# A decoder layer stack: softmax sums of the first attention taken from the value products, and plain downward products in the last expert stage

## The reference, cut to what matters

```python
# first sub-layer: 16 heads of 8 values, B = 4 batches, T = 512 tokens
qkv = layernorm(x) @ W_attn + b_attn                      # q, k, v
att = einsum('bqhd,bkhd->bhqk', q, k) * scale / temperature
att = where(causal, att + slope[h] * (k_pos - q_pos), -inf)
w = softmax(att)                                          # exponentials divided by their sum
x = x + einsum('bhqk,bkhd->bqhd', w, v) @ W_proj + b_proj
...
# last sub-layer: 32 experts of width 64, 4 for each token, the weights are given in bfloat16
h = silu(xe @ W1) * (xe @ W3)
ye = h @ W2                                               # the downward product
x = x + sum over experts of weight * ye + silu(x @ sw1.T) * (x @ sw3.T) @ sw2.T
```

## Time and profile before

| | us |
|---|---|
| median of three runs | 2444.63 |
| lowest, highest | 2435.88, 2444.8 |
| the profiled execution | 2446.44 |
| its span | 2444.7 |

### The profile page before, as it was taken

The page is one execution under the profiler, slowest core; times in us unless marked ns, Lnnn a source line. Parts: engine busy times, 40 slices in busy tenths (PEclk is TensorE's granted clock), DMA queues, the critical chain, the costliest instruction groups (busy, mean ns, idle before and its releaser), DMA issues. The chain is left out here.

```text
span 2444.7 us, 37814 instructions
## 1 busy us (share of the span) xinstructions
PE 2141.9 (88%) x12822; PEld 1482.2 (61%) x12822; DVE 1735.3 (71%) x3653; ACT 1214.2 (50%) x2508; POOL 1174.9 (48%) x1354
## 2 busy tenths in 40 slices
PE   6998779578999976658999999999999977869888
PEld 3666557455788854455666666666666645548655
DVE  5778678655788865665777777778766764479498
ACT  6888545223566652234444444544444433444455
POOL 5332028001699940117766776667665610004298
PEclk8999889867999988768999999999999998989899
DMA  1000015000766600012442434333433331000184
GB/s 49 2 3 2 7 48 123 7 6 21 172 154 153 155 21 20 1 68 39 89 102 74 105 72 106 76 102 82 93 91 73 83 78 41 0 1 1 41 180 108
DMA packets 64904, 161.92 MB, mean 66 GB/s; under 512 B 7995, under 2 KB 19003, under 8 KB 57416
## 3 DMA queue, kind: packets, MB, share of 16 engines
q1 hardware_dynamic: 64712, 159.50, 27.7%
HBM read 156.46 MB, written 3.01 MB: 65 GB/s over the span
## 5 line engine op out<-in xcount | busy, mean ns | idle before, releaser
L2361 PE MATMUL bank<-l2h_og,l2h_wo 128*128 128x512 f32 x512 | 260.2, 593 | 1.6 <-DVE LNT L2622 1.6
L2471 ACT ACTIVATE l2h_pr<-twin,l2h_nmx 128x512 f32<-128x512 f32 x256 | 176.0, 688 | 152.1 <-PE bank L2350 105.4
L2463 ACT ACTIVATE l2h_prT<-bank 128x512 f32<-128x512 f32 x256 | 151.6, 592 | 195.0 <-PE bank L2350 195.0
L1177 POOL TENSOR_TENSOR l1m_hid_lo<-l1m_hid,l1m_hid_hi 128x512 fp32r<-128x512 f32 x128 | 209.5, 1657 | 46.4 <-ACT l1m_hid_hi L1110 46.1
L2625 DVE TENSOR_REDUCE l2h_nmx<-twin 128x2 f32<-128x1024 f32 x128 | 156.0, 1219 | 93.3 <-PE twin L2339 93.2
L2700 POOL TENSOR_TENSOR l2h_vs<-l2h_vg 128x256 f32<-128x256 f32 x256 | 192.9, 753 | 20.3 <-DVE l2h_vg L2598 20.3
L2598 DVE TENSOR_TENSOR l2h_vg<-bank,l2h_gv 128x512 f32<-128x512 f32 x256 | 174.6, 682 | 34.4 <-POOL l2h_vs L2700 21.8
L2610 DVE TENSOR_TENSOR l2h_og<-bank,l2h_gt 128x512 f32<-128x512 f32 x256 | 172.8, 678 | 3.8 <-PE bank L2361 2.7
L2695 POOL TENSOR_TENSOR l2h_plain<-l2h_plain,l2h_rotated 128x512 f32<-128x512 f32 x64 | 82.5, 1289 | 172.9 <-DVE l2h_rotated L2591 172.9
L2350 PE MATMUL bank<-ident,l2h_pr 128*128 128x128 f32 x1024 | 160.8, 280 | 0.0
L2350 PEld LDWEIGHTS bank<-ident,l2h_pr 128*128 128x128 f32 x1024 | 116.7, 140 | 66.8 <-issue 43.1
(11 more groups left out here) (608 smaller groups left out, 5940.1 us busy)
## 6 DMA issues: line engine op xcount, KB each, us to landing
l2h_gt<-l2m_gate_rows SPq DMA_DIRECT2D x128, 512.0 KB, 7.4
l1m_c<-l1m_weights SPq DMA_DIRECT2D x62, 512.0 KB, 6.5
l3m_c<-l3m_weights SPq DMA_DIRECT2D x30, 512.0 KB, 6.6
l0m_c<-l0m_weights SPq DMA_DIRECT2D x14, 512.0 KB, 6.7
l1m_w<-in_l1m_pairs SPq DMA_DIRECT2D x32, 192.0 KB, 6.5
l2h_fresh<-in_l2m_wqkv SPq DMA_DIRECT2D x8, 768.0 KB, 4.3
l2h_wo<-in_l2m_wo SPq DMA_DIRECT2D x8, 512.0 KB, 3.8
l0m_w<-in_l0m_pairs SPq DMA_DIRECT2D x8, 192.0 KB, 5.7
```

What stands on the lines that cost most here:

```text
L1177: nc.gpsimd.tensor_tensor(hid_lo[:, h % RING, :], hid[:, h % 4, :], hid_hi[:, h % RING, :], ALU.subtract)\
L2361: nc.tensor.matmul(ybank[:, :], wo[s][:, e, :], og[:, e % 4, :], start=(e == 0), stop=(e == E - 1))\
L2463: nc.scalar.activation(prT[:, j // 2 % 2, h, :, j % 2 * P:(j % 2 + 1) * P], tbank[:, :].rearrange("p (c q) -> p c q", c=TPB), ACT.Copy).th ...
L2471: nc.scalar.activation(pr[:, h, :], sbank[:, h, :], ACT.Exp, bias=nmx[:, k % 2, h:h + 1], accum_out=rs[:, g % 2, t, h:h + 1]).then_inc(exp ...
```

## The change

In the first attention:

- The cell of a head in `v` is now 32 columns wide (8 values, 8 ones, 16 zeros). One product of 32 columns gives both the weighted values and the sums, and L494 is gone. Groups 0 and 1 go to the first 128 columns of `obank`, groups 2 and 3 to the second.
- After each fourth quad, ScalarE copies `obank` to `raw_y`, three iterations after the quad. VectorE no longer inverts and multiplies there.
- Once for each batch, in iterations 2 to 6 of the next: TensorE picks the sums (`sum_rows`, 8 products, iteration 2), VectorE inverts 64 columns and spreads them to 1024 (iteration 3), TensorE brings the factors to their places (`spread_rows`, four products each in iterations 4 and 5), VectorE multiplies (two 128x512 products, iterations 4 and 5, between the second and the third mask), and TensorE projects with a padded `wproj` in eight products in place of four (`put_out`, iteration 6). VectorE adds to x in iteration 7 in place of 3, and FIRST is 7 in place of 4: the pieces stand in iterations 7 to 15.
- Quads of 128 or 256 keys share copies: four heads, or two, are turned into one bank and copied by one instruction of 512 columns. In a quad of 128 keys ScalarE and VectorE take turns from quad to quad.

In the last expert stage, even steps (`whole(h)`) take hid in float32 and the downward weights widened to float32 by ScalarE (`widen_down`, 128x128) in one plain product. Their rounding and subtraction are gone, and odd steps stay as they were. `hid` has 8 buffers in place of 4. l0m and l1m keep their work.

```diff
-    FIRST = 4
+    FIRST = 7
...
+            wide = max(1, R // (tt + 1) // 2 * 2) if tt < 2 else 1
...
-                    if 0 <= j < QUADS and j % G == G - 1:
...
-                        nc.vector.reciprocal(rinv[:, :], obank[:, P:2 * P]).then_inc(inverted, 1)
...
+                    ended, late = divmod(k - PER, PER)
+                    if ended >= 0 and late == 3:
+                        dve.wait_ge(summed, ended + 1)
+                        nc.vector.reciprocal(rinv[:, :], pbank[:, 0:TPB * 4 * R]).then_inc(inverted, 1)
...
                     if k < QUADS:
                         mask(k, 0)
                     if 1 <= k <= QUADS:
-                        copy(k - 1, 1)
+                        copy(k - 1, 0)
                     if k < QUADS:
-                        for r in range(1, R):
+                        mask(k, 1)
+                    if ended >= 0 and late in (4, 5):
+                        half = late - 4
+                        ts = slice(2 * half, 2 * half + 2)
+                        dve.wait_ge(factored, 2 * ended + half + 1)
...
-                    if k >= PER and k % PER == 3:
+                    if k >= PER and k % PER == 7:
...
+                    if j >= 0 and j % G == G - 1:
+                        b, tt, _ = place(j)
+                        act.wait_ge(pv_done, j + 1)
+                        if b:
+                            act.wait_ge(yT_ready, 2 * b)
+                        nc.scalar.activation(raw_y[:, tt, :, :], obank[:, 0:2 * P].rearrange("p (s q) -> p s q", s=2), ACT.Copy)\
+                            .then_inc(raw_taken, 1)
...
-                            out = nc.tensor.matmul(obank[m, P:2 * P], ones[:, g * R * HD:(g + 1) * R * HD],
-                                                   prT[:, j % RING, r, t * P:(t + 1) * P], start=False, stop=end)
+                            m, c = slice(32 * r, 32 * r + 32), r * G * CELL + side * 2 * CELL + odd * 2 * HD
+                            out = nc.tensor.matmul(obank[m, side * P:(side + 1) * P], v[:, b % 2, t, c:c + CELL],
+                                                   prT[:, j % RING, r, t * P:(t + 1) * P], start=first, stop=end)
                     out.then_inc(pv_done, 1)
...
+        def whole(h):
+
+            return half_weights and h % 2 == 0
...
+                    if whole(h):
+                        if blk == 0:
+                            pe.wait_ge(w_whole[s], turn + 1)
+                        pe.wait_ge(hidden, PRE + h + 1)
+                        out = nc.tensor.matmul(acc[blk][:, :], w_down[s][:, :], hid[:, h % HELD, :], start=False, stop=h >= STEPS - B)
```

More of the change, by code:

```diff
@@ L255, in piece_at, with by_scalar, unit_of, copies_until @@
             return [(b + 1, n - FIRST)] if b + 1 < B and 0 <= n - FIRST < PIECES else []
+        def by_scalar(tt, g, u):
+            return g % 2 == 0 if tt == 0 else u % 2 == 0
+        units, on_a, on_v = [], 0, 0
+        for k in range(QUADS):
+            _, tt, g = place(k)
+            wide = max(1, R // (tt + 1) // 2 * 2) if tt < 2 else 1
+            mine = []
+            for u in range(R // wide):
+                scalar = by_scalar(tt, g, u)
+                on_a, on_v = on_a + scalar, on_v + (not scalar)
+                mine.append((slice(u * wide, (u + 1) * wide), scalar, on_a if scalar else on_v))
+            units.append(mine)
+        units_before = [sum(len(u) for u in units[:k]) for k in range(QUADS + 1)]
+        def unit_of(k, r):
+            return units_before[k] + [n for n, (heads, _, _) in enumerate(units[k]) if heads.start <= r < heads.stop][0]
+        def copies_until(k, scalar):
+            return max([0] + [n for q in units[:k + 1] for _, s, n in q if s == scalar])
+        def fbank(b, half):
+            return sbank[0] if half and b + 1 == B else pbank
         def home(b, n):
@@ new lines, in weigh, with sum_rows @@
+                    out.then_inc(pv_done, 1)
+                def sum_rows(b):
+                    pe.wait_ge(raw_taken, TPB * b + TPB)
+                    if b + 1 < B:
+                        pe.wait_ge(v_ready, b + 2)
+                    else:
+                        pe.wait_ge(added, b)
+                    for t in range(TPB):
+                        for side in range(2):
+                            out = nc.tensor.matmul(pbank[:, t * 4 * R:(t + 1) * 4 * R], raw_y[:, t, side, :], sums_of[:, side, :],
+                                                   start=(side == 0), stop=(side == 1))
+                    out.then_inc(summed, 1)
@@ new lines, in spread_rows @@
+                def spread_rows(b, half):
+                    pe.wait_ge(widened, b + 1)
+                    if half and b + 1 < B:
+                        pe.wait_ge(yT_ready, 2 * b + 1)
+                    for t in range(2 * half, 2 * half + 2):
+                        for side in range(2):
+                            at = (2 * (t % 2) + side) * P
+                            out = nc.tensor.matmul(fbank(b, half)[:, at:at + P], factor[:, t, side, :], T.ident[:, :], start=True, stop=True)
+                    out.then_inc(factored, 1)
@@ L497, in _, with put_out @@
+                def put_out(b):
+                    pe.wait_ge(yT_ready, 2 * b + 2)
+                    for t in range(TPB):
+                        for side in range(2):
+                            out = nc.tensor.matmul(pbank[:, t * D:(t + 1) * D], yT[:, t, side, :], wproj[:, side, :], start=(side == 0),
+                                                   stop=(side == 1))
+                    out.then_inc(out_ready, 1)
                 pe.wait_ge(loaded, 16 * len(loads))
@@ L1135, in _ @@
                         split_weights(g, 0)
+                    if g < SLOTS - 1 and half_weights:
+                        widen_down(g, 0)
                 for c in range(B):
```

215 lines of the change are left out of this document (129 added, 86 removed).

## The result

The changed kernel takes **2464.2 us** (median of 4 runs, 2460.4 to 2465.7) against 2441.9 for the kernel before (4 runs, 2435.9 to 2444.8). The ratio is 1.0091, with a 95% interval from 1.0074 to 1.0107. It is slower by 22 us, where 6 us less were forecast, and it lies 14 us above the upper end of the range, 2450.

The account below looks back on a forecast made before the run. Nothing was taken to bound the kernel as a whole. First attention +3.3 and last expert stage -9.5 sum to -6.2 us: 2446.4 becomes 2440.2, the median 2438.4, with a range from 2425 to 2450.

Parts of the forecast that it names:

- The last stage: Last expert stage: 1.80 to 1.64 us a step over 56 steps, 0.5 at the end; -9.5 us, between -13 and 0.
- Rival (c): Last expert stage doesn't move, VectorE staying at 1.8 us a step: 2448 us; chance 0.14.
- the layout of quads 4 and 5: First attention, batches two and three: hand layout from score to score, quad 4 at 3.85 us, quad 5 at 4.25.
- the gain put on shared copies: First attention, narrow quads: shared copies take two or three fixed parts out of a quad; 0.8 us in the first batch.
- batches two and three: First attention: -0.7 for quads 0 to 6, +1.5 for quad 7, +0.65 for the widest; +1.4 us each, +2.8 together.
- first batch: First attention: loses three pieces from narrow quads (1.6), gains 0.8 through shared copies, pays 0.65; -2 us.
- last batch: First attention, no pieces: first eight quads 23.7 + 2.8, 384-key quads 13.3, three of 512 keys 11.2; -2.1 us.
- end of the stage: First attention's tail: 10.2 us where it was 3.3, last three weighings giving 2.3 back; +4.6 us.
- Rival (b): First attention: VectorE stands at `factored`, ScalarE runs empty, each refill 1 us more in quads 2 to 7; 2456 us; chance 0.08.
- Rival (a): First attention: shorter TensorE queue felt everywhere, a batch sheds 3 us more; -8 there, -17.5 in all, 2427 us; chance 0.28.
- the distance of those quads is ScalarE's: First attention, 384-key quads with pieces: ScalarE has no slack, TensorE has; they stay at 16.2 us for four.
- The widest: First attention, four 512-key quads of a middle batch: ScalarE's work with moved pieces takes them from 18.0 to 18.65 us.

Follow-up runs that it names:

- e1: Kernel before's first attention with the changed kernel's last expert stage: 2431.5 us, ratio 0.9959 to before.
- e9: Changed kernel with VectorE's factor product behind the four masks and single copies in place of shared ones: 2439.4 us, ratio 0.9982 to before.
- e6: Changed kernel plus four zero-weight filler products on TensorE at the end of narrow quads 2, 3, 4, 6, 7 and 0 of a batch: 2463.4 us.
- e8: Kernel before with the changed kernel's shared narrow copies alone: 2450.8 us, ratio 1.0040 to before.
- e3: Changed kernel without shared copies, every head's turned weights copied singly: 2451.1 us, ratio 1.0039 to before.
- e5: Changed kernel with VectorE's factor product behind the four masks instead of between second and third: 2451.9 us, ratio 1.0048 to before.
- e4: Changed kernel with zero-weight products in place of the products with ones it lost: 2471.3 us, ratio 1.0117 to before.
- e2: Kernel before with FIRST = 7 in place of 4, so projection pieces stand later, nothing else: 2452.9 us, one run.

## Why the prediction was wrong

**The last stage: right, a little small.** Forecast were 9.0 us in the 56 steps and 0.5 at the end. The 56 steps gave 11.1 and 11.9 us in the traces of the changed kernel and of e1, that is 1.60 and 1.59 us a step; with the first eight steps it is 12.8 and 11.8, and 11.0 by the medians. The forecast's figure for TensorE alone was 1.58 a step and 12.3 us, and in the stretches shown TensorE is busy for 20.00 of 20. So most of the allowance of 0.06 us a step for VectorE and TensorE waiting for each other wasn't needed, since the product with the routing weight runs at 692 ns in the median and not at 1065. The rule of an exclusive lock (the Trainium skill, SBUF — State Buffer, section Who interferes with whom) would ask 1.26 + 2 x 0.69 = 2.64 us of a pair for the subtraction and the two products with the routing weight. That is an estimate from the page's rule and the shortest durations of the earlier trace rows; it is under TensorE's 3.16, so these runs can't tell that rule from a milder one. Rival (c) fell.

**The first attention: the steps that failed are the layout of quads 4 and 5, whose wait for the factors was priced at the full clock, and the gain put on shared copies.** By the prediction's terms, with the kernel that has both edits (e9) beside the changed one:

| term | forecast | changed kernel | e9 |
|---|---|---|---|
| batches two and three, each, to before | +1.4 | +7.2, +7.0 | +1.1, +1.4 |
| first batch | -2.0 | +4.8 | -2.4 |
| last batch | -2.1 | +7.8 | +0.8 |
| end of the stage | +4.6 | +5.8 | +7.9 |

- Quads 4 and 5 were laid out at 3.85 and 4.25 us. In batches two to four they took 5.85 and 5.95 to 6.54. The prediction names the wait ("behind VectorE's second mask stands the product that waits for `factored`") and prices it at the full clock, where quad 5 of e6 confirms it (4.32). At the lower level, the four products that spread the factors take 2.08 us and a score 0.58 (at the full clock 1.06, in e6, and 0.38), the whole loop from TensorE to VectorE and back is that much longer, and nothing covers it.
- "Shared copies are in that: they take two or three fixed parts out of a quad." They take out 0.0 to 0.3 us of four quads at the full clock (e8, and the changed kernel beside e9) and cost 13.0 in the changed kernel by the medians (e3) and 12.5 beside the product moved (e9 and e5), since each makes masks wait for more turns. In the traces of e3 and e9 the largest part of that is in the first batch.
- No term and no rival had the granted clock in it. The quads were laid out with durations at 1.00, and in quads 4 to 7 the change left idle time that the trace of before didn't have (TensorE idle for 5.0 of 21.2 us, from 2.0 of 14.6).
- Rival (b) was the case that came, with 0.08. Its mechanism, VectorE standing at `factored` with two masks undone, was worth 12.3 us (e5); its place was mostly two quads, not six, and its price there 1.1 to 2.3 us a quad rather than 1 (e5 beside the changed kernel). Its argument against, that narrow quads have idle time already, was wrong: the idle time was the same loop.
- Rival (a) was wrong in quads with pieces: those of 384 keys stayed at 16.2 in the first batch and with both edits come to 16.0 (e9), a few tenths from before. But TensorE does count in them, which "the distance of those quads is ScalarE's" leaves out: with zero products added they take 17.5 at a clock of 1.00 (e4), and in batches two and three of the changed kernel they took 17.3 and 17.1, with clocks of 0.92 and 0.94.

**What held.** Quads 0 to 3: 11.7, laid out at 11.8; there the sum is partly luck, since quad 2 took 3.7 for 3.1 and quad 3 took 2.3 for 3.1. Quads of 384 keys: 16.2 at the full clock. The widest: 18.9, forecast 18.65. Quad 6 and 7 of batch three: 3.9 and 5.6, forecast 3.8 and 4.9. Once both waits are gone, a middle batch costs 1.1 to 1.4 us (forecast 1.4), with the quads of 384 keys 0.2 shorter and the widest 0.9 longer.

**Mis-sized.** The last batch: its quads of 384 keys were to take 13.3 and took 15.1 to 15.5, more than before, and the three widest 12.65 instead of 11.2; the products that went gave those quads little or nothing. The end of the stage: 10.8 us from the copy to the last add's end, forecast 10.2. Picking took 1.96 (forecast 2.0), inverting and spreading 1.3 (1.9), but the factors were late, at the lower clock, 1.9 us to the first product (1.2) and 1.7 more to the second (0.95). In e9 the projection too was at the lower level, 12.9 us in all.

**The sum.** 32.7 us of loss in the first attention are 24.8 for the two waits (2464.2 to 2439.4) and 8.0 for the rest (2439.4 to 2431.5), against 3.3 forecast. Taken each against the runs of before beside it, the rest is 9.6 us (1.3 and 11.0 below before), so it is known to some 2 us. The term that was mis-sized there is the end of the stage, with +7.9 in e9 for +4.6.

**What stays open.** Why the clock falls. The wait for the factors didn't start it, since the fall came first, at the end of quad 3 or the start of quad 4. With both waits gone (e9) it still falls there, for a shorter time. What in quad 3 does it isn't separated: the projection that went to iteration 6, the products with ones, and the inversion with its copy ahead of the masks were not put back one by one; and e8, which has none of these three, also lost the clock in quad 3 of two batches. Shown is what goes with it: the same instructions took 2.8 us more in four quads at a lower clock (e2) and 1.07 more in one (e6), and with the product behind the masks the clock was 0.78, 0.84 and 0.79, from 0.75, 0.74 and 0.63 (e5). Filler brought the clock back in two batches of four and gained nothing in the sum. Why the last batch of e2 ran at 0.66 with work unchanged wasn't found.

## What to carry to other kernels

- An instruction that waits for TensorE belongs behind those that TensorE's next work waits for. In a chain of handovers its place in the queue was worth 12 us, for an instruction of 0.7 us that stands among masks six times.
- Fewer, larger copies help an engine that is full. In stretches where the engines wait for each other they lengthen the wait for the first result; here they cost 9 to 13 us and gained 0.3 in four quads at most.
- Where a change takes work off TensorE in a stretch that isn't TensorE's, price that stretch a second time with the durations at the lower clock (here turns of 0.25 us instead of 0.14), and give that case a chance of its own.

## What the hardware showed that was not expected

- The granted clock can't be read off the busy time of a stretch. It was 0.75 in batch two's quads 4 to 7 with TensorE busy for 16.2 of 21.2 us (76%), and 1.00 in the last batch's quads of 384 keys of the kernel with single copies, with 10.9 of 15.1 us (72%).
- A product with 16 columns of output costs nearly what one with 128 does, both in float32 with weights of 128x128 and at a granted clock of 1.00: the eight that pick the sums take 1.96 us (16 records, two for each product), the eight of the projection with 128 columns take 2.05.
- Spreading 64 columns to 1024 on VectorE took 0.69 us, as long as a product of 512 columns with two inputs, where I had put 1.2.
